# A new order of splits and products within a step: the b parts behind the layer-0 coefficients

## The reference, cut to what matters

```python
def layer(x, A, B, ids, W, b, experts, router):
    u = (x @ B[ids].T) @ A[ids].T                    # adapter of each sequence, rank 16
    alpha = softmax(router_bias + u @ router.T)      # 4 experts (bias in layer 0 only)
    mix = sum(2 * alpha[e] * (u @ EA[e].T) @ EB[e].T for e in range(4))   # rank 8 each
    return u @ W.T + b + mix
x = x + layer0(x, ...)    # 8 adapters, chosen by itok_B_3_7
x = x + layer1(x, ...)    # 64 adapters, chosen by itok_B_4_50
```

## Time and profile before

| | us |
|---|---|
| median of three runs (lowest, highest) | 335.08 (334.63, 335.91) |
| the profiled execution | 334.41 |
| its span, first to last instruction | 332.7 |
| TensorE busy | 307.0 (92%) |
| VectorE busy | 220.1 (66%) |
| ScalarE busy | 186.4 (56%) |
| GpSimd busy | 63.3 (19%) |
| mean granted TensorE clock, share of full speed | 0.995 |

### The profile page before, as it was taken

The page is one execution under the profiler, slowest core; times in us unless marked ns, Lnnn a source line. Parts: engine busy times, 40 slices in busy tenths (PEclk is TensorE's granted clock), DMA queues, the critical chain, the costliest instruction groups (busy, mean ns, idle before and its releaser), DMA issues.

```text
span 332.7 us, 6476 instructions
## 1 busy us (share of the span) xinstructions
PE 307.0 (92%) x2048; PEld 284.4 (85%) x2048; DVE 220.1 (66%) x476; ACT 186.4 (56%) x384; POOL 63.3 (19%) x58
## 2 busy tenths in 40 slices
PE   5994998799989998999979999999999999999894
PEld 4453998589978998999979999999999999899783
DVE  2156887686738766686658666777668676864556
ACT  1446976946546565755466465646575657461520
POOL 5600000620042103320143003320332024200000
PEclk9999899999999999999999999999999999999999
DMA  7999973006870388126840587037811783041006
GB/s 267 345 365 381 347 208 156 0 8 167 300 224 0 104 243 302 51 60 212 286 139 0 158 284 250 2 103 244 299 47 55 255 292 92 0 193 62 1 0 252
DMA packets 30773, 56.16 MB, mean 169 GB/s; under 512 B 3633, under 2 KB 20050, under 8 KB 30754
## 3 DMA queue, kind: packets, MB, share of 16 engines
q1 hardware_dynamic: 29666, 52.97, 48.3%
q0 software_dynamic: 1088, 2.97, 2.5%
HBM read 39.15 MB, written 16.78 MB: 168 GB/s over the span
## 4 chain that ended last, share of the span: by engine, by line
issue 41%; PE 20%; DMA 13%; POOL 12%; DVE 6%; ACT 3%; SPq 2%; POOLq 1%; DVEq 0%; ACTq 0%
POOL xs_lo L952 8%; DMA out<-xraw 6%; DMA xraw<-x_in 6%; PE ps_d L307 3%; PE ps_d L309 3%; PE ps_d L308 3%; POOL a1s_lo L952 2%; DVE xs_lo L740 2%; DVE xraw L942 2%; PE ps_d L545 1%; PE ps_p L307 1%; PE ps_d L547 1%; ACT res L574 1%; SPq L253 1%; SPq L251 1%
## 5 line engine op out<-in xcount | busy, mean ns | idle before, releaser
L952 POOL TENSOR_TENSOR xs_lo<-xraw,xs_hi 128x512 fp32r<-128x512 f32 x28 | 36.0, 1290 | 182.5 <-ACT xs_hi L574 182.4
L307 PE MATMUL ps_d<-w1s_hi,a1s_hi 128*128 128x384 f32 (+1 forms) x192 | 63.9, 333 | 0.0
L309 PE MATMUL ps_d<-w1s_hi,a1s_lo 128*128 128x384 f32 (+1 forms) x192 | 62.0, 323 | 0.0
L308 PE MATMUL ps_d<-w1s_lo,a1s_hi 128*128 128x384 f32 (+1 forms) x192 | 61.9, 322 | 0.0
L942 DVE SCALAR_TENSOR_TENSOR xraw<-ps_d,lp,xraw 128x512 f32<-128x512 f32 x60 | 43.6, 748 | 22.5 <-PE ps_d L547 22.5
L574 ACT ACTIVATE xs_hi<-xraw 128x512 fp32r<-128x512 f32 x60 | 36.0, 626 | 26.4 <-DMA xraw<-x_in 25.9
L307 PE MATMUL ps_p<-xs_hi,bst_hi 128*128 128x256 f32 x120 | 36.5, 304 | 6.2 <-DVE bst_lo L740 2.4
L308 PEld LDWEIGHTS ps_d<-w1s_lo,a1s_hi 128*128 128x128 f32 x192 | 36.2, 189 | 0.0
L307 PEld LDWEIGHTS ps_d<-w1s_hi,a1s_hi 128*128 128x128 f32 x192 | 36.1, 188 | 0.0
L309 PEld LDWEIGHTS ps_d<-w1s_hi,a1s_lo 128*128 128x128 f32 x192 | 36.1, 188 | 0.0
L308 PE MATMUL ps_p<-xs_lo,bst_hi 128*128 128x256 f32 x120 | 34.5, 288 | 0.0
(11 more groups left out here) (227 smaller groups left out, 702.9 us busy)
## 6 DMA issues: line engine op xcount, KB each, us to landing
out<-xraw SPq DMA_DIRECT2D x31, 512.0 KB, 3.5
xraw<-x_in SPq DMA_DIRECT2D x28, 512.0 KB, 5.0
w_plain<-w SPq DMA_DIRECT2D x16, 512.0 KB, 8.9
abraw<-ab_tab SPq DMA_DIRECT2D x64, 128.0 KB, 2.1
b0raw<-b_tab SPq DMA_DIRECT2D x64, 64.0 KB, 2.0
xraw<-x_in POOLq DMA_DIRECT2D x4, 512.0 KB, 11.0
a_plain<-a SPq DMA_DIRECT2D x1, 512.0 KB, 3.6
out<-xraw SPq DMA_DIRECT2D x2, 256.0 KB, 2.7
```

The lines of the kernel that those rows point to most:

```text
L307: pe.matmul(acc, lh, rh, start=first, stop=False, skip_group_check=True)
L308: pe.matmul(acc, lh, rl, start=False, stop=False, skip_group_check=True)
L309: return pe.matmul(acc, ll, rh, start=False, stop=final, skip_group_check=True)
L952: return pool.tensor_tensor(dst, whole, high.bitcast(F32), ALU.subtract)
```

## The change

The order within a step is changed on three engines; no instruction is added or removed.

- TensorE, steps 1 to 7: of part 0 only three chunks stand before the transposes of `h`; the other five and two chunks of part 1 follow `route(0)`; the other six of part 1 follow `turn()`; all of part 2 stands behind `query()`. In the last step four result tiles and not five stand before the second `turn()`.
- ScalarE: the b quarters and part 0's high half stand behind the coefficients of layer 0 (`coef_high(0)`), then come all four x chunks of half 0, part 1's high half, layer 1's coefficients, part 2's high half and the four x chunks of half 1.
- VectorE: softmax is first, with the `ht` low parts inside it between the subtraction and the sum; the b quarters and part 0's low half stand behind the coefficients of layer 0; part 1's low half behind layer 1's coefficients.
- GpSimd's and SyncE's programs are as before.

```diff
@@ TensorE @@
                     after_step(pe, d_out, KT * g)
-                    wide(0)
+                    wide(0, range(3))
...
                 route(0, f0x)
-                if not first:
-                    wide(1)
-                wide(2, range(KT // 2))
+                if first:
+                    wide(2, range(KT // 2))
+                else:
+                    wide(0, range(3, KT))
+                    wide(1, range(2))
                 pe.wait_ge(ht_lo, g + 1)
...
                 turn()
-                wide(2, range(KT // 2, 3 * KT // 4 if last else KT))
+                if first:
+                    wide(2, range(KT // 2, KT))
+                else:
+                    wide(1, range(2, KT))
...
                 query()
-                if last:
-                    wide(2, range(3 * KT // 4, KT))
+                if not first:
+                    wide(2)
...
-                    start_results((0, 1, 2, 3, 4))
+                    start_results((0, 1, 2, 3))
@@ ScalarE @@
-                if not last and not first:
-                    act.wait_ge(h_done, g + 1)
-                    split_b(g + 1)
...
-                wide_high(0)
                 act.wait_ge(ht_done, g + 1)
...
-                if not last and not first:
-                    split_x(g + 1, 1 - par, 0, [0, 1])
                 softmax_exp(0)
-                wide_high(1)
...
                 coef_high(0)
-                if first:
-                    split_b(g + 1, QUARTERS[0:2])
+                wide_high(0)
                 if not last:
-                    split_x(g + 1, 1 - par, 0, range(CH) if first else [2, 3])
-                wide_high(2)
-                if first:
-                    split_b(g + 1, QUARTERS[2:4])
+                    split_b(g + 1, QUARTERS[0:2] if first else QUARTERS)
                 if not last:
-                    split_x(g + 1, 1 - par, 1, [0])
+                    split_x(g + 1, 1 - par, 0)
+                wide_high(1)
...
+                wide_high(2)
+                if first:
+                    split_b(g + 1, QUARTERS[2:4])
                 if not last:
-                    split_x(g + 1, 1 - par, 1, range(1, CH))
+                    split_x(g + 1, 1 - par, 1)
                 softmax_exp(1)
@@ VectorE @@
-                if not last and not first:
-                    split_b(g + 1)
...
+                    if layer == 0:
+                        dve.wait_ge(ht_hi, 2 * g + 2)
+                        low(ht[:, 1, :], ps_t[:, 0:P], ht[:, 0, :])
+                        low(he[ELO, :], ps_t[0:LR, P:2 * P], he[0:LR, :]).then_inc(ht_lo, 1)
...
+                softmax(0)
+                coef_low(0)
+                if not last:
+                    split_b(g + 1, (0, 1) if first else range(4))
                 wide_low(0)
-                dve.wait_ge(ht_hi, 2 * g + 2)
-                low(ht[:, 1, :], ps_t[:, 0:P], ht[:, 0, :])
-                low(he[ELO, :], ps_t[0:LR, P:2 * P], he[0:LR, :]).then_inc(ht_lo, 1)
-                softmax(0)
-                wide_low(1)
-                coef_low(0)
-                if first:
-                    split_b(g + 1, (0, 1))
...
+                wide_low(1)
                 if first:
                     split_b(g + 1, (2, 3))
```

More of the change, by code:

```diff
@@ L531, in body @@
                 if last:
-                    from_layers(5)
-                    from_layers(6)
+                    for m in (4, 5, 6):
+                        from_layers(m)
                 else:
```

## The result

The change makes the kernel slower: 341.28 us, median of four runs (339.88 to 342.45), against 335.5 us (334.63 to 336.36) of the kernel before. The ratio is 1.0198, with a 95% interval of 1.0152 to 1.0243: slower, and whether by more or less than 2% stays open. The forecast was 339.6 us (336.4 to 342.8) and slower. The sign was right, and so were the loop (the ring) over x, gathers and stores and the late start of GpSimd; GpSimd's hold on VectorE came in half of the steps only; and the size was too small (+1.98% where +1.35% was forecast). Throughout, ratios leave out runs that are more than 1.5% above the fastest of their kernel, which concerns one run of the experiments (346.13 us) and two of the kernel before.

The account below looks back on a forecast made before the run. The prediction took a loop over x, A split, gathers, store and load (35.0 us), nearly tied with TensorE (34.5), as the bound. Terms +5.0, +1.0, +0.8 and -2.1 made +4.7 us; forecast 339.6 us, range 336.4 to 342.8.

Parts of the forecast that it names:

- the ring: Loop from x chunk 3's copy through A split, gathers, store and load to the next chunk 3: 35.0 us, about a step.
- GpSimd's hold on VectorE: GpSimd's fourth x split stretches the low half of layer 1's coefficients on VectorE; the pair goes from 0.87 to about 1.6 us.
- step 0: First step: part 0's high half ahead of b and x delays the x splits; +1.0 us, between 0 and +2.
- five turns of the ring: Chunk 3 of step 1 to that of step 6, each turn +1.0 us: +5.0 us.
- last stretch: Last `h` product to the end: `query` before all of part 2 covers a 2.07 us wait; 34.88 to 32.8 us, -2.1.
- The wait before `turn(0)`: TensorE's wait for VectorE's softmax before layer 0's transposes, 6.2 us over six times; goes, but isn't subtracted from the time.
- The walk behind `turn(0)`: Work after layer 0's transposes: first projection waits 0.43 and 0.47 us for GpSimd, `route(1)` 0.56; TensorE's step 36.8 us.
- the ring's first leg: From the copy of x chunk 3 to the end of the A part's split: 10.9 us instead of 9.8, +1.0 a step.
- The first (327): Rival, the gain stands: the loop has slack, so 6.2 + 2.1 us go; 327 us, chance 6%.
- The second (a wash, 335.2): Rival: first leg grows by only 0.2 us, or store and load take 0.5 less; 335.2 us, chance 12%.
- The third (no hold, 336.9): Rival: VectorE's coefficient low half runs beside GpSimd's splits, +0.5 us a turn; 336.9 us, chance 12%.
- The fourth (343, more than one hold): Rival: VectorE's b splits and GpSimd's x splits take turns, +1.6 us a turn; 343 us, chance 10%.

Follow-up runs that it names:

- the first experiment: Kernel before, with ScalarE making layer 0's exponential ahead of the copy of x chunk 1, not behind it: 334.83 us, ratio 0.9985.
- the kernel without the ring: Changed kernel, with SyncE's stores and loads issued between its gathers instead of behind all 16: 338.44 us, ratio 1.0074.
- the fastest kernel: Changed kernel with part 0's halves early, SyncE's stores between its gathers, and part 1's low half ahead of layer 1's coefficients on VectorE: 323.02 us, ratio 0.9642.
- the kernel with the filled stops: Changed kernel, with matmuls of unused result in TensorE's stops in the first projection and before `route(1)`, steps 1 to 6: 340.34 us, ratio 1.0192.
- the second experiment: Kernel before, with the changed order in step 7 only, on TensorE, ScalarE and VectorE: 330.37 us, ratio 0.9874.

## Why the prediction was right in sign and low in size

The terms of the sum, in us, by the two profiled executions (334.41 and 342.45):

| term of the prediction | forecast | measured |
|---|---|---|
| start, to the first `h` | 0 | +0.25 |
| step 0 | +1.0 | +1.72 |
| first `h` of step 1 to its x chunk 3 | 0 | -0.91 |
| five turns of the ring | +5.0 | +6.61 |
| chunk 3 of step 6 to the last `h` | +0.8 | +2.71 |
| last stretch | -2.1 | -2.38 |
| sum | +4.7 | +8.00 |

The medians give a smaller miss: 341.28 - 335.5 = +5.8 us, where 339.6 against 335.08 was +4.5. The profiled execution of the kernel before has one of the highest mean clocks of that kernel's runs, and that of the changed kernel the lowest of four, so some 2 us of the +8.00 lie in which executions were profiled.

**The wait before `turn(0)` goes, and the gain is given back.** Right. It went in the changed kernel (6.2 to 0.3) and in the first experiment (6.2 to 0.9), where the ratio was 0.9985. The ring holds in the kernel before: it was lengthened by 1.3 us and steps 4 to 6 became 0.3 to 1.1 us longer; it was shortened, with the exponential first, and they became 0.6 us shorter.

**The walk behind `turn(0)`.** Right in place, and near in size. The stops came at chunks 2 and 3 of the first projection and before `route(1)`. GpSimd's four splits took 5.26 us (forecast 4 × 1.27), the ring's first leg 10.72 in steps 1 to 3 (forecast 10.9, before 9.8 to 9.95), and step 4, which neither the ring nor the clock lengthened, 36.55 (forecast 36.4 to 36.8); the kernel without the ring gave 36.61.

**The hold by GpSimd.** Right in steps 4 to 6, where the coefficient pair took 2.16, 1.53 and 1.85 us (forecast 1.6, before 0.87), and absent in steps 1 to 3, where it took 0.87. The rule of the Trainium skill's page "SBUF — State Buffer", section "Who interferes with whom", agrees with the traces: 0.87 us for the pair with GpSimd idle, 1.53 where its first half meets the last split, and 2.38 in the fastest kernel, where the pair comes due earlier in the row of splits. What was wrong is when the pair comes due. I had x chunk 3 at 8.5 us behind the start of `turn(0)`, from step 5 of before; in steps 1 to 3 it was copied 9.1 to 9.3 us behind it, and ScalarE's half of the pair was made when GpSimd was through (step 1: last split to 102.91, pair from 103.00).

**The first leg came out near its forecast for another reason.** In steps 1 to 3, where the ring decides, it grew by 0.8 to 0.9 us without the hold; my sum without a hold had +0.5. I walked the leg over VectorE: held coefficients, then part 1's low half. The traces show it on ScalarE: behind chunk 3 stand part 1's high half, the coefficients and part 2's high half, and only then the x chunks of half 1, 3.5 us behind the start of chunk 3 in the changed kernel. Their low parts start with the end of the first of them (105.11 in step 1), 0.1 us after VectorE is through with part 1's low half. The two engines are almost tied there. The experiment that takes part 1's low half out of VectorE's queue shows which of them sets the leg, for it stays at 10.7 us. So the +1.0 a turn was close to right partly by luck.

**What failed: "Steps 4 to 6 at 36.4 to 36.8 us each".** Step 4 was (36.55). Steps 5 and 6 took 37.73 and 37.54, because the granted clock fell to 0.50 in the second projection. The sum has no term for that. The clock of before (0.995 in the mean, 1.00 in every stretch of the earlier trace rows) gave no sign in the one profile that I had, and I priced each stop at its own length and 0.08 us for the restart. The price of a fall is 0.92 to 1.2 us a step where TensorE sets the step: 1.2 and 1.0 in steps 5 and 6, and about 1 us in step 0, whose clock was 0.92 and which came out 0.7 above its term. These three make some 2.9 us, against 3.3 that were missing in the pair of profiles; the other misses of the table (+0.25 in the start, -0.91 before chunk 3 of step 1, -0.28 in the last stretch, and what is left of the ring's turns) nearly cancel. In steps 1 and 3 the fall is partly hidden by the ring: those two took 37.98 and 38.05, and step 1 of the kernel with the filled stops took 37.78 with the clock at 1.00. How much of the +5.8 us of the medians is the clock's can't be read by step; the median of the mean clocks is 0.978 for the changed kernel's four runs and 0.987 for the kernel before.

**A smaller miss in the same part.** I had the ring and TensorE tied in all six steps. In steps 1 to 3 they were. In steps 4 to 6 the ring has slack after the change: x chunk 3 lands before GpSimd is through with the chunks in front of it, and the leg measured from its copy is then 11.3 to 11.9 us, most of it GpSimd's queue. GpSimd's late start and TensorE set the step there.

**The last step.** Right: -2.38 of -2.1 forecast, and it stands alone, as the second experiment shows.

**The rivals.** The first (327) fell with the first experiment. The second (a wash, 335.2) needs a first leg that grows by only 0.2 us; it grew by 0.8 to 0.9. The third (no hold, 336.9) had its condition met in steps 1 to 3 and not its price of +0.5 a turn, so it missed the time, though not for the hold that it leaves out. The fourth (343, more than one hold) gives a time near the measured one, but for another reason: GpSimd's row of splits started when forecast and ran in 5.26 us, so it wasn't pushed back.

What stays open: why the clock falls in some steps and not in others with the same stops (steps 2 and 4 in the changed kernel, four of six in the kernel without the ring), and what a held clock is worth in the timed runs, which four runs of the kernel with filled stops could not show.

## What to carry to other kernels

In a kernel with a period, add up the legs of every loop through buffers and queues before pricing a wait: a wait of 6.2 us that TensorE named was worth nothing (0.9985), while an issue order on SyncE, which no view of busy time shows, held a loop as long as the step. When work is moved behind a point, read the other engine's queue there: here four splits that had been spread over 10 us came in a row, and a coefficient pair came late, held by them in some steps and by ScalarE's queue in others; the operations queued behind that pair, not the pair, were what TensorE missed. And count the stops that a change makes as well as their length: those of step 5 (1.5 us between starts beyond the pitch) were followed by a stretch at half the clock that cost about 1 us more.

## What the hardware showed that was not expected

**The clock can fall behind short stops.** In step 5 TensorE stopped for 0.23, 0.27 and 0.54 us (by the brackets of the timeline; 0.38 to 0.70 between starts beyond the pitch) within 3 us, and from 255.93 the granted clock was 0.50 for 3.2 us. With matmuls in the stops it stayed at 1.00 in steps 1 to 6. The same stops did not always do it: steps 2 and 4 of the changed kernel had them without a fall. Nor is a row of stops needed. In the kernel before, single stops of up to 1.7 us before `turn(0)` were followed by no fall; a stop of 2.07 us before `route(1)` of the last step was followed by a fall in one profile (the exponential first, 7 us at 0.50) and by none in two others; and one of 2.41 us before the first projection of the start was followed by a fall in 11 of the 13 profiles. What decides between them is not shown. The Trainium skill's page "TensorE: Matmul & The Clock Gate", section "A second HAM failure mode: psum-queue depth-cycling", describes short idle moments between groups of matmuls that make the clock go back and forth; these runs agree that it can happen, with the numbers above.

**The issue of a small transfer.** On SyncE, 16 gathers take 8.5 us before the first store, 0.5 us each, for 64 or 128 KB each; four transfers of 4 bytes took 1.2 to 1.3 us, 0.3 each. That is long enough to set the time of a step.
